# Cross attention, FFN and top-2 experts on one core: norms moved to GpSimd, two blocks' list scatters issued together, weight pieces and routing steps moved

## The reference

```python
x = x + _L0_xattn_ref(_layernorm(x), ctx_1024, w1, b1, w2, b2, g1, beta1, g2, beta2, g3, beta3)
x = x + _L0_ffn_ref(_layernorm(x), wg, w1, w3, w2)

def _L0_xattn_ref(y, Z, ...):                  # y: 2048 x 256, Z: 1601 x 256
    sa = attention(y, y, y, causal=True)
    y = layernorm(y + sa, g1, beta1)
    ca = attention(y, Z, Z, causal=False)
    y = layernorm(y + ca, g2, beta2)           # "the cross norm"
    h = relu(y @ w1 + b1)                      # 256 -> 1024
    y = layernorm(y + h @ w2 + b2, g3, beta3)  # "the output norm"
    return y

def _L0_ffn_ref(x, wg, w1, w3, w2):            # x: "the h norm" of the sum so far
    probs = softmax(x @ wg.T)                  # 8 experts
    topk_w, topk_idx = top_k(probs, 2)         # weights renormalised to sum 1
    y_e = (silu(x @ w1[e].T) * (x @ w3[e].T)) @ w2[e].T      # 256 -> 512 -> 256
    return sum over the 2 chosen e of weight_e * y_e
```

## Time and profile before

| | us |
|---|---|
| median of 3 executions | 590.29 |
| the three | 590.04, 590.29, 596.56 |
| the profiled execution, its own time | 598.84 |
| its span, first to last instruction | 597.1 |
| PE busy | 516.4 (86%) |
| DVE busy | 388.5 (65%) |
| ACT busy | 292.0 (49%) |
| POOL busy | 249.5 (42%) |
| mean granted TensorE clock | 0.96 |

### The profile page before, as it was taken

One profiled execution on the slowest core, in us unless ns is written; L12 is line 12 of the kernel. 1 busy time (PEld: TensorE's weight loads), 2 busy tenths in 40 slices (PEclk: granted clock), 3 DMA queues, 4 the chain that ended last, 5 costly groups with the idle time before them and its releaser, 6 DMA issues. The chain is left out here.

```text
span 597.1 us, 11431 instructions
## 1 busy us (share of the span) xinstructions
PE 516.4 (86%) x3824; PEld 339.9 (57%) x3824; DVE 388.5 (65%) x1010; ACT 292.0 (49%) x588; POOL 249.5 (42%) x255
## 2 busy tenths in 40 slices
PE   4999999898999996994969939887998898899992
PEld 2676666565666754672645627653664455555561
DVE  5899784787966888665586777878554343334441
ACT  3656766464675455643156336553643243334340
POOL 3645040052323121442124243654457655657664
PEclk9999999999999997997898987998989999999997
DMA  7031613468672357129374076307958686668783
GB/s 255 2 99 38 202 54 124 89 139 163 141 121 71 76 121 175 55 63 75 66 165 107 22 58 213 125 2 113 140 96 96 65 141 107 115 119 118 128 129 40
DMA packets 130421, 63.12 MB, mean 106 GB/s; under 512 B 104733, under 2 KB 121694, under 8 KB 130366
## 3 DMA queue, kind: packets, MB, share of 16 engines
q1 hardware_dynamic: 121854, 52.13, 42.2%
q0 software_dynamic: 8512, 10.26, 12.2%
HBM read 28.23 MB, written 10.54 MB: 65 GB/s over the span
## 5 line engine op out<-in xcount | busy, mean ns | idle before, releaser
L1038 PE MATMUL ps<-arena,probT 128*128 128x256 f16 (+2 forms) x1092 | 187.5, 327 | 21.7 <-DMA probT<-prob 12.7
L1038 PEld LDWEIGHTS ps<-arena,probT 128*128 128x128 f16 (+1 forms) x1092 | 108.4, 100 | 83.9 <-issue 24.9
L863 ACT ACTIVATE prob<-ps,nbias 128x512 f16<-128x512 f32 x64 | 39.0, 609 | 76.4 <-DVE nbias L1533 70.3
L817 POOL DMA_INDIRECT out<-y,qst x39 | 62.7, 1607 | 23.9 <-issue 13.2
L1038 PE MATMUL ps<-arena,qT 128*128 128x512 f16 (+1 forms) x384 | 69.5, 332 | 3.6 <-DVE prob L1668 3.4
L2001 DVE SCALAR_TENSOR_TENSOR ps<-ps,w1m 128x512 f32<-128x512 f32 x39 | 27.3, 699 | 67.0 <-ACT w1m L994 59.5
L994 ACT ACTIVATE w1m<-ps 128x512 f32<-128x512 f32 x39 | 23.3, 597 | 96.0 <-PE ps L1038 78.2
L1038 PE MATMUL ps<-probT,w1m 128*128 128x512 f16 (+1 forms) x192 | 48.1, 352 | 17.6 <-DVE prob L1668 8.7
L1038 PE MATMUL ps<-arena,tT 128*128 x468 | 58.6, 276 | 0.0
L1038 PEld LDWEIGHTS ps<-arena,qT 128*128 128x128 f16 x384 | 32.5, 97 | 37.9 <-issue 4.8
L1038 PE MATMUL ps<-tT 128*128 128x512 f16 (+3 forms) x240 | 51.6, 354 | 1.8 <-DVE tT L1495 1.8
(11 more groups left out here) (183 smaller groups left out, 940.4 us busy)
## 6 DMA issues: line engine op xcount, KB each, us to landing
stage<-we_in SPq DMA_DIRECT2D x33, 256.0 KB, 3.1
prob<-we_in SPq DMA_DIRECT2D x15, 256.0 KB, 5.0
xin<-x_in SPq DMA_DIRECT2D x4, 512.0 KB, 6.0
out<-y SPq DMA_DIRECT2D x4, 512.0 KB
hrow<-tT SPq DMA_DIRECT2D x4, 512.0 KB
y<-x_in SPq DMA_DIRECT2D x3, 512.0 KB, 6.4
stage<-z_in SPq DMA_DIRECT2D x4, 256.0 KB, 5.3
prob<-w_in SPq DMA_DIRECT2D x4, 256.0 KB, 3.1
```

What stands on the lines that cost most here:

```text
L817: g.indirect_dma_start(out[:rows_of(p), :], bass.IndirectOffsetOnAxis(rec[:, n, 0:1], 0), ys[:, n % RING, :], None, compute_op=ALU.add).th ...
L863: a.activation(row_cols(q, 0, c), ps[c][:, :w], ACT.Exp, bias=nbias[:, q, :], scale=SM)
L1038: r = t.matmul(o, lhs(a), rhs(b), start=first and n == 0, stop=last and n == 2)
```

## The change

- **Three norms on GpSimd.** The cross norm's subtract-and-scale of all 16 tiles moves from DVE (`c_norm`) into POOL's `ln_affine`; `residual` waits on DVE until POOL has read the buffer (`c_nrm`). For blocks 0 to 2 the output norm (`out_norm`: power, four `tensor_scalar`, one multiply and one add of 128 x 1024) and the h norm (`h_norm`: power, four `tensor_scalar`) are POOL's.
- **Scatters.** `scatter(0)` and `scatter(1)` both stand in step i = 13, behind a wait for tile 14's last transpose (`c_t02`). Before they stood in steps 9 and 13. `scatter(2)` keeps its place in POOL's order, but its slots are made later.
- **Weight pieces.** The first six of `rest` are loaded in step 13, in front of the transposes of tile 15; places are renumbered.
- **Block 3's FFN.** `y_trans(3)` goes ahead of `c_pv(14)`, `y_hi(3)`, `y_lo(3)` between the exponentials and low halves of tile 15; `c_pv(15)` comes after `down(3, 1)` where it stood after `up(3, 1)`.
- **Routing of block 2.** `h_hi`, `h_lo`, `h_trans`, `logits` move from unit 3 to unit 4, `choose(2)` behind all of unit 4's `hid_lo`, `gates(2)`, `routed(2)`, `table_starts(1)` and `table(1)` behind it, into the first two expert tiles.
- **End of block 3.** `moments`, `centre` from ahead of the loop to tile 2, `first_out`, `x1_stats` to tile 3, `h_norm` to tile 4; the three places become 6, 7, 8.

```diff
-        H_AT, LOGITS_AT, RANKS_AT = 5, 6, 7
+        H_AT, LOGITS_AT, RANKS_AT = 6, 7, 8
...
@@ SP
                     loads(chunk_from(u), chunk_from(u) + len(CHUNK_PIECES[u]))
+                    if u == 2:
+                        for m in range(6):
+                            rest_load(sp, m)
...
-            store_x1(sp, 2)
...
             for m in range(PLACES, len(rest)):
                 rest_load(sp, m)
+            store_x1(sp, 2)
             store_h(sp, 2)
...
                 if n == 1:
+                    store_x1(sp, NB - 1)
+                if n == 2:
                     lists_ready(1)
...
@@ POOL
             def ln_affine(pre, i, q, row):
+                pool.wait_ge(sm[pre + "rstd"], i + 1)
+                g.tensor_scalar(nrm[:, q, :], u[:, q, :], mv[:, q, 0:1], rstd[:, q, :], ALU.subtract,
+                                ALU.mult).then_inc(sm[pre + "nrm"], 1)
...
+            def out_norm(j):
+
+                rstd_of("n_", j)
+                wait(pool, "n_rstd", j + 1)
+                for m in range(TB):
+                    g.tensor_scalar(blk(j)[:, m, :], blk(j)[:, m, :], mv4[:, m, 0:1], rstd4[:, m:m + 1],
+                                    ALU.subtract, ALU.mult).then_inc(sm["n_nrm"], 1)
+                wait(pool, "n_nrm", TB * (j + 1))
+                g.tensor_tensor(blk(j), blk(j), bc(0), ALU.mult).then_inc(sm["n_gam"], 1)
+                wait(pool, "n_gam", j + 1)
+                wait(pool, "f_xb", j + 1)
+                g.tensor_tensor(blk(j), blk(j), xin[:, j % 2], ALU.add).then_inc(sm["n_x1"], 1)
+
+            def h_norm(j):
+
+                rstd_of("m_", j)
+                wait(pool, "m_rstd", j + 1)
+                if j:
+                    wait(pool, "r_logit", j)
+                for m in range(TB):
+                    g.tensor_scalar(h4[:, m, :], blk(j)[:, m, :], mv4[:, m, 0:1], rstd4[:, m:m + 1],
+                                    ALU.subtract, ALU.mult).then_inc(sm["m_h"], 1)
...
-                if i == NT - 1:
-                    rstd_of("m_", 2)
+                if i - 3 in FIRST and i != NT - 1:
+                    h_norm(FIRST[i - 3])
                 ln_rstd("c_", i, i % 2)
+                ln_affine("c_", i, i % 2, 2)
                 if i - 1 in FIRST:
-                    rstd_of("n_", FIRST[i - 1])
-                if i - 3 in FIRST:
-                    rstd_of("m_", FIRST[i - 3])
-                ln_affine("c_", i, i % 2, 2)
+                    out_norm(FIRST[i - 1])
                 if i in FIRST:
                     j = FIRST[i]
                     y_b2(j)
                     x_beta(j)
-                    if j:
-                        scatter(j - 1, range(TB))
-            pool.wait_ge(sm["c_y"], NT)
+                    if j == 2:
+                        pool.wait_ge(sm["c_t02"], 16 * (NT // 2))
+                        scatter(0, range(TB))
+                        scatter(1, range(TB))
+            h_norm(2)
             x_beta(NB - 1)
             y_b2(NB - 1)
...
@@ PE
-            y_trans(3, NT - 1)
             up(3, 0)
             up(3, 1)
-            c_pv(NT - 1)
...
             down(3, 1, i)
+            c_pv(NT - 1)
             up(3, 5)
...
             up(4, 4)
+            h_trans(2, 0)
             down(4, 2, i)
             up(4, 5)
+            h_trans(2, 1)
             down(4, 3, i)
             up(4, 6)
+            logits(2)
...
             down(4, 6, i)
+            ranks(2)
+            counts(1)
             down(4, 7, i)
...
@@ DVE
-                if i - 2 in FIRST:
-                    centre(FIRST[i - 2])
                 if i - 3 in FIRST:
-                    first_out(FIRST[i - 3])
-                    x1_stats(FIRST[i - 3])
                     x1_aggr(FIRST[i - 3])
...
+            for m in range(TB):
+                x1_stats(2, m)
+            x1_aggr(2)
             y_lo(4)
             rest_lo(dve, REST_AT[3][KF - 1])
             for m in range(2):
                 out_tile(NB - 1, m)
             for f in range(KF):
                 hid_lo(4, f)
...
+            choose_read(2)
+            choose(2)
+            place_read(2)
+            table_counts(1)
             for m in range(2, TB):
                 out_tile(NB - 1, m)
```

151 lines of the change are left out of this document (64 added, 87 removed).

## The result

The changed kernel takes 597.77 us (median; 593.35 to 605.47) where the kernel before, timed beside it, takes 592.54: a ratio of 1.0092, 95% interval 1.0062 to 1.0121. It is 0.9% slower, clear of the noise, but inside the 2% that the text ahead calls no change. 579 was forecast, and the range ended at 594.

The account below looks back on a forecast made before the run. PE was taken as bound by DVE's softmax turn and norms, scatter 0's DMA stall and the late `y_lo(3)`. 598.84 - 3.3 - 1.0 - 15.4 + 2.4 + 4.0 = 585.5; from the median, 590.3 - 11.3 = 579.0; range 565 to 594.

Parts of the forecast that it names:

- the cross stage: Block stretches before unit 2: norms off DVE gain 3.3 us, slow clock 1.0, scatter 0 leaving step 9 15.4.
- the head: Start of block 3 up to the loop: earlier `y_lo(3)` gains 0, loop's first matmul comes 2.4 us later.
- the loop: Expert loop: block 2's scatter runs into it, meeting activation transposes and delaying gathers 4 and 5; 4.0 us lost.
- the step from the profiled execution to the median: Whole kernel: 2 us less gain counted in a median execution, as step 11's stall is likeliest to vary; 11.3 us.
- The block stretches: Blocks 0 and 1, sign of being right: both stretches equal, 34 to 35 us, instead of 37.60 and 49.70.
- POOL's `tensor_scalar`: Norms on POOL: 0.73 us per instruction, taken from a `tensor_tensor`; bounds half and twice that.
- rival D: Tile 15's transposes: sixteen scatters reach them, or step 11's stall wasn't theirs; 12.1 us come back, 591 us; chance 0.15.
- Rival B: Head of block 3 keeps its gain, the 8.65 us wait for `y_lo(3)`: 570 us; chance 0.23.
- The weight pieces: DVE's weight pieces in unit 3: each 0.68 us plus 0.4 for conflict with POOL's norms.
- The end of block 3, a tile later throughout, keeps its distance to tile 17, which needs it: 0: Expert loop: moving block 3's end a tile later costs 0 us.
- rival C: Scatter's collision moves to loop tiles 0 to 3; loop loses 15 to 20 us, 596 us; chance 0.12.
- A loop over 10 us longer: Expert loop, sign of being wrong: it takes over 10 us longer than before.

Follow-up runs that it names:

- b_pool_norms: Kernel before, with only the norms of all cross tiles and the output and h norms of blocks 0 and 1 on GpSimd: 577.21 us, 0.9803.
- b_both: Kernel before plus GpSimd norms (cross tiles, blocks 0 and 1) and block 0's scatter moved to step 13; head and loop as before: 572.91 us, 0.9734.
- x_after: The changed kernel itself, unaltered, timed a second time on another chip: 593.50 us, 1.0087.
- a_tiles_late: Changed kernel, with block 3's first two output tiles on DVE put behind the fourth `hid_lo` of unit 4: 589.03 us, 0.9984.
- x_end3: Changed kernel, with block 3's end back at the turns of the kernel before, on the chip of `x_after`: 589.59 us, 1.0018.
- x_both: Same kernel as `b_both`, a third time, on the chip of `x_after`: 570.82 us, 0.9683.
- a_sc_back: Changed kernel, with block 0's scatter back in step 9: 597.24 us, 1.0067.
- d_pieces: `b_both` plus the change's places for the last weight pieces, six of them loaded in step 13: 585.96 us, 0.9898.
- the hybrid: Kernel of `b_both`: the change's cross stage without its early weight loads, with the head and loop of before; 0.9734, 0.9823 and 0.9683 in three runs.
- d_y3: `d_pieces` plus block 3's first transposes and their split in step 14, as in the change: 586.01 us, 0.9886.
- r_both: Same kernel as `b_both`, a second time, on another chip: 584.85 us, 0.9823.
- r_end3: `b_both` with block 3's end one turn later as in the change, on the chip of `r_both`: 594.67 us, 0.9999.

## Why the prediction was wrong

Against the profiled execution before, the sum had -19.7 for the cross stage, +2.4 for the head and +4.0 for the loop. Measured are -18.45, +9.9 and +11.1. Two steps failed: the head, where tile 15's transposes had no price, and the loop, where block 3's later end had none. Beside them, the step from the profiled execution to the median took 2 us off a gain; measured were +2.5 us between the profiled executions and +5.2 between the medians.

**The cross stage: right.** Unit 2 was to start 19.7 us earlier and starts 18.45 earlier. The wait for `probT<-prob` in step 11 is gone but for 0.73 us. The block stretches, 34 to 35 us and equal as forecast, are 34.57 and 34.56, and the wait for the low half is 2.43 us in the first, against about 2.5.

**POOL's `tensor_scalar`: undersized.** 0.73 us was taken. By line, in the changed kernel (busy, mean ns, idle before):

```profile
L707 POOL TENSOR_SCALAR nrm<-u,mv,rstd 128x256 f32<-128x256 f32 x16 | 20.5, 1281 | 1.7
L777 POOL TENSOR_SCALAR tT<-y,mv,rstd 128x256 f32<-128x256 f32 x12 | 15.3, 1288 | 0.3
```

1.28 us, inside the bounds. The four of `h_norm(2)` take 4.98 us where 2.9 were forecast, 2.1 us more on the head's chain. It costs nothing in the cross stage: `b_pool_norms` gains 2.0%.

**The head, the first step to fail: "The six early weight loads stand on SP in front of tile 15's transposes; unit 2 hides them", and of these transposes "It met tile 15's transposes before and will again", without a price.** The forecast times (`c_pv(15)` "from about 358.7 to 364.5" and what follows), less the 18.45 by which unit 2 starts earlier, can be laid beside the measured ones:

| | forecast, us | measured, us | later by |
|---|---|---|---|
| `c_pv(15)` starts | 340.3 | 345.1 | 4.9 |
| `c_pv(15)` ends | 346.1 | 352.0 | 5.9 |
| moments of block 2 | 352.6 | 358.3 | 5.8 |
| `y_b2(3)` ends | 361.9 | 369.3 | 7.5 |
| `hid_lo(4, 0)` | 362.8 | 370.1 | 7.3 |
| the loop's first matmul | 379.8 | 387.3 | 7.5 |

PE was ready for `c_pv(15)` at 340.7, about as forecast, and waited 4.44 us for tile 15's transposes. `c_pv(15)` then took 6.9 us, at a granted clock of 0.63, where 5.8 were forecast. So nearly all of the 5.8 us was lost in this one place; most of the other 1.7 is POOL's price. From there on the chain went as described: DVE stood 9.42 us for `y_b2(3)`, and PE 9.06 us in front of `down(4, 0)`. The chain was the right one, and what entered it came late.

The transposes, and the weight loads of step 13 ahead of them, in the changed kernel:

```profile
L552 SPq DMA_TRANSPOSE probT<-prob x3: 1234/2616/11060, 328.8 to 341.8; - x3
...
DMA to landing us min/median/max: 5.8/16.2/16.7
```

```profile
L387 SPq DMA_DIRECT2D stage<-we_in x2: 328/488/647, 316.8 to 319.4; - x2
...
DMA to landing us min/median/max: 14.2/24.1/24.7
```

and the same transposes in `b_both`, with the same sixteen scatter DMAs up to the same time (329.93), but without the six loads:

```profile
L550 SPq DMA_TRANSPOSE probT<-prob x3: 1247/1282/2072, 328.1 to 331.1; - x3
...
DMA to landing us min/median/max: 6.5/7.0/7.3
```

The three of the six loads whose landing the trace shows land 14.2 to 24.7 us after their issue, the last at 344.1; SP is held 11.06 us by the second transpose, and all three land between 345.0 and 347.6. In the four traces with sixteen scatters and the six loads (the change, `x_after`, `a_tiles_late`, `x_end3`) the first two transposes take 14.5 to 16.7 us to land; with the scatters alone (`b_both`, `x_both`) 6.4 to 8.5; with the loads and eight scatters (`a_sc_back`) 5.6 to 7.9. By these traces it takes both together. No run has the loads as its only edit without the unshown waits: in `d_pieces` the transposes are issued at 338, when the scatter is over, and land in 3.1 to 4.0. In `b_both` the last transpose lands at 338.40 and `c_pv(15)`, at its old place, starts at 340.79: nobody waits for it.

So rival D named the right place, but its mechanism, that the scatters reach so far, isn't what the hybrids show, and its "12.1 come back" was wrong: the wait is 4.44 us. Rival B's wish, to keep that 8.65, did not come true even in `d_y3`.

**The weight pieces, 0.4 us more each in my sum, had no part in it.**

```profile
L398 DVE SCALAR_TENSOR_TENSOR arena<-prob,arena x7: 678/693/1229, 335.1 to 370.8; 128x512 f16<-128x512 f32 x7
```

The median is 0.69 us, as before. POOL and DVE where they met, in order of time:

```profile
335.22 1.70 POOL L707 TENSOR_SCALAR nrm<-u,mv,rstd 128x256 f32<-128x256 f32 x1
336.07 0.71 DVE L398 SCALAR_TENSOR_TENSOR arena<-prob,arena 128x512 f16<-128x512 f32 x1
337.00 0.72 POOL L710 TENSOR_TENSOR nrm<-nrm,vec 128x256 f32<-128x256 f32 x1
337.04 1.23 DVE L398 SCALAR_TENSOR_TENSOR arena<-prob,arena 128x512 f16<-128x512 f32 x1
```

Beside POOL's `tensor_tensor` the piece is the longer one (1.23 us; another has 0.87), beside the `tensor_scalar` POOL's instruction is (1.70 us instead of 1.22), and most of what the norms added is `tensor_scalar`. The rule of the Trainium skill (Advanced Engine Details and Errata, GPSIMD Details), that the Pool engine conflicts with DVE instructions that have two SBUF inputs, agrees with the earlier trace rows and with the 1.23 us here, and carried no weight in the result.

**The loop, the second step to fail: "I take 4.0 us", and "The end of block 3, a tile later throughout, keeps its distance to tile 17, which needs it: 0".** Measured were 11.1 in this pair of executions, and 6.6 as a mean over the twenty traces. I looked at tile 17, the consumer, and not at what the moved steps hold up in the queues: SP's third transpose (10 us later) and POOL's gather of tile 4 (5.78 us of wait on PE, 4.17 in `x_after`). Both stood in my text, the first under rival C, which named "SP's `act_turn(2)` also stands behind `store_x1(3)`" and asked 15 to 20 us for it, with the collisions of transposes and scatter. What the runs show in place of the 0: block 3's later end alone costs 9.8 us in the hybrid (`r_both` to `r_end3`, one chip) and 3.9 in the change (`x_end3` to `x_after`, one chip). C's side was right, and its mechanism in part: the queue is held as it said, but PE's direct wait for transposes is 0.70 us in the change. A loop over 10 us longer was among my signs of being wrong, and it came in the first pair. C's deciding point, a loop loss of 11.3 us, was nearly met, but the head's 9.9 did as much.

**What the change is worth by parts.** On chips without the unshown waits: norms of the tiles and of blocks 0 and 1 on GpSimd -2.0%, both scatters together -0.7 to -0.9%, block 3's end +0.7%. With the unshown waits: block 3's end +1.8% in the hybrid, and, across chips, block 2's late routing +1.5 to +2.2%, the moved weight pieces about +0.7%. What is left of the 4% between the hybrid and the change lies in block 2's norm on GpSimd with `y_b2(3)` behind it, of which the order of two output tiles alone gives back 1%, and in the late transposes of tile 15. I have no run of either alone, so this split is argued and not shown.

The hybrid, 572.91 and 570.82 us (0.9734 and 0.9683), beats both kernels; with the unshown waits it is still at 0.9823.
